# Graph layer on Trainium2: normalising two steps behind the statistics, ten loads issued by GpSimd, the first layer's bounds inside the input block, keys and values four chunks sooner

## The reference, cut to what matters

```
xn  = layernorm(x)
x0  = relu(gat(xn; W1, att1) + b1)        # 4 heads, softmax over the edges of each destination
x2  = gat(x0; W2, att2) + b2
mix = linear attention on xn: k, v normalised per head, dots = k^T v, q @ dots / N, then Wout, bout
x   = x + x2 + mix
x   = x + layernorm(x + top-2-of-16 experts(layernorm(x))) * gamma + beta
```

## Time and profile before

| | us |
|---|---|
| median of 3 runs (lowest, highest) | 2814.59 (2810.1, 2815.09) |
| the profiled execution | 2810.95 |
| its span, from first to last instruction | 2809.0 |
| POOL busy | 1864.1 (66%) |
| PE busy | 2204.9 (78%) |
| DVE busy | 1825.2 (65%) |
| ACT busy | 932.2 (33%) |
| largest group: 1568 gathers L957 | 1488.1, 949 ns each, 495.5 idle before them |

### The profile page before, as it was taken

How to read it: one execution, slowest core, us unless ns; L and a number is a source line. 1 busy time by engine, 2 the same in 40 slices (tenths; PEclk the granted TensorE clock), 3 DMA queues, 4 the chain that set the end, 5 groups by cost and what they waited for, 6 DMA issues and landing times. The chain is left out here.

```text
span 2809.0 us, 54426 instructions
## 1 busy us (share of the span) xinstructions
PE 2204.9 (78%) x11643; PEld 1733.5 (62%) x11644; DVE 1825.2 (65%) x4373; ACT 932.2 (33%) x2266; POOL 1864.1 (66%) x1942
## 2 busy tenths in 40 slices
PE   4638777777778777658888888888888479999986
PEld 3426555555555555446666666666666269999975
DVE  4767777777777777476666666666666565555546
ACT  3403333333333333202222222222222144444436
POOL 1447777777777777467777777777777126666654
PEclk9869999999999999879999999999999689999998
DMA  5535555555555555376565655565656345565546
GB/s 184 171 97 149 146 145 146 146 146 146 146 145 146 146 147 143 79 225 161 157 164 156 163 154 164 157 161 156 163 153 160 90 128 101 103 104 105 101 85 189
DMA packets 262987, 402.24 MB, mean 143 GB/s; under 512 B 78879, under 2 KB 175542, under 8 KB 262904
## 3 DMA queue, kind: packets, MB, share of 16 engines
q0 software_dynamic: 102880, 254.96, 36.8%
q1 hardware_dynamic: 122376, 105.98, 13.9%
q10 hardware_dynamic: 37663, 40.56, 4.4%
HBM read 347.09 MB, written 54.62 MB: 143 GB/s over the span
## 5 line engine op out<-in xcount | busy, mean ns | idle before, releaser
L957 POOL DMA_INDIRECT gathered<-table,idx x1568 | 1488.1, 949 | 495.5 <-issue 453.6
L1288 PE MATMUL psA_e<-scaled,hotf 128*128 128x260 f32 x3136 | 746.5, 392 | 44.0 <-issue 39.4
L1288 PEld LDWEIGHTS psA_e<-scaled,hotf 128*128 128x128 f32 x3136 | 589.4, 193 | 131.8 <-issue 48.2
L1159 ACT ACTIVATE scaled<-t_e 128x32 f32<-128x32 f32 x196 | 45.0, 230 | 733.8 <-DVE t_e L1021 722.9
L1691 POOL DMA_INDIRECT moe_d<-xscaled,xtarget x113 | 179.2, 1586 | 124.5 <-DVE xtarget L1635 52.0
L1032 DVE TENSOR_TENSOR scaled<-gathered,psDW_e 128x2048 f32<-128x2048 f32 x98 | 223.6, 2282 | 25.4 <-ACT psDW_e L1160 25.4
L1025 DVE TENSOR_TENSOR hotf<-psA_e,code_r 128x1024 f32<-128x1024 f32 x196 | 239.7, 1223 | 0.1
L1032 DVE TENSOR_TENSOR scaled<-gathered,psW_e 128x2048 f32<-128x2048 f32 x98 | 223.6, 2282 | 22.4 <-ACT psW_e L1160 22.4
L1663 PEld LDWEIGHTS xpsH<-xxT,w1e 128*128 128x128 f32 x1808 | 220.6, 193 | 6.1 <-ACT xxT L1592 0.4
L1672 PE MATMUL xpsO<-w,hidT 128*128 x904 | 216.8, 383 | 7.7 <-DVE hidT L1624 6.9
L1663 PE MATMUL xpsH<-xxT,w1e 128*128 128x128 f32 x1808 | 221.3, 276 | 0.0
(11 more groups left out here) (322 smaller groups left out, 3381.2 us busy)
## 6 DMA issues: line engine op xcount, KB each, us to landing
w<-codes_d SPq DMA_DIRECT2D x196, 256.0 KB
gathered<-table,idx POOLq DMA_INDIRECT x1592
w<-in_L_ffn_w ACTq DMA_DIRECT2D x8, 2048.0 KB, 19.1
xb<-in_L_ffn_b SPq DMA_DIRECT2D x113, 128.0 KB
table<-acc POOLq DMA_DIRECT2D x49, 130.0 KB
table<-acc ACTq DMA_DIRECT2D x49, 130.0 KB
xnT_d<-w SPq DMA_DIRECT2D x49, 128.0 KB, 2.5
w<-xnT_d SPq DMA_DIRECT2D x49, 128.0 KB, 3.8
```

The lines of the kernel that those rows point to most:

```text
L957: pool.indirect_dma_start(out=G[:, q, k, :], out_offset=None, in_=table, in_offset=bass.IndirectOffsetOnAxis(ap=idx[:, q, k:k + 1], axis=0 ...
L1159: act.activation(scaled[:, par, :, C:GW], t[:], ACT.Exp).then_inc(s["weights"], 1)
L1288: ins = pe.matmul(psA[:, q, 0:GW], hotf[:, q, k, :], scaled[:, par, k, :], start=(k == 0), stop=(k == KT - 1))
```

## The change

In `inputs`: (1) the normalising, and with it transpose, copy, store and product, stand one turn later. (2) Ten of the thirteen transfers move from ACT's list to POOL's, ahead of POOL's table stores; the same ten lines are gone from ACT's. (3) The body of `bounds` becomes a function, and for the first layer it runs at the end of DVE's list in the input block (with its two PE instructions at the end of PE's); the block `bounds` 0 is gone. In `gat_edges` 0: (4) all steps of keys and values have offsets smaller by four.

```diff
-                stage(bounds, 0, ident, ones, acc, dtab, own, peak, parts, wide, table[0], idx, G, firsts[0], None)
...
-            tiles(sp, (0, load), (3, store_x))
+            tiles(sp, (0, load), (4, store_x))
...
+            pool.wait_ge(s["filled"], 2)
+            pool.dma_start(by_chunk_i[0:FULL, :], a["dst"][0:FULL * CE].rearrange("(k e) -> k e", e=CE)).then_inc(s["dst_in"], 16)
+            pool.dma_start(by_chunk_i[FULL:NC, 0:REST * KT], a["dst"][FULL * CE:E].rearrange("(k e) -> k e", k=1)).then_inc(s["dst_in"], 16)
+            pool.dma_start(srcp[E:NC * CE].rearrange("(p t) -> p t", t=KT), zero_i[0:P - REST, :]).then_inc(s["src_stored"], 16)
+            pool.dma_start(srcp[0:E].rearrange("(p f) -> p f", p=P // 4), a["src"].rearrange("(p f) -> p f", p=P // 4)).then_inc(s["src_stored"], 16)
+            pool.dma_start(wkv[:], a["L0_mix_Wqkv"][MI:3 * MI, :].rearrange("(k p) c -> p k c", p=P)).then_inc(s["w_mix_in"], 16)
+            pool.dma_start(wout[:], a["L0_mix_Wout"].rearrange("(k p) c -> p k c", p=P)).then_inc(s["w_mix_in"], 16)
+            pool.dma_start(wq, a["L0_mix_Wqkv"][0:MI, :].rearrange("(k p) c -> p k c", p=P)).then_inc(s["w_mix_in"], 16)
+            pool.dma_start(wext1[:, :, 0:C], a["L0_gnn_W2"].rearrange("(k p) n -> p k n", p=P)).then_inc(s["w1_in"], 16)
+            pool.dma_start(att1[:, 0, :], a["L0_gnn_att_src2"].rearrange("(o h) c -> o (h c)", o=1).to_broadcast([P, C])).then_inc(s["w1_in"], 16)
+            pool.dma_start(att1[:, 1, :], a["L0_gnn_att_dst2"].rearrange("(o h) c -> o (h c)", o=1).to_broadcast([P, C])).then_inc(s["w1_in"], 16)
...
-            tiles(dve, (1, normalise), (0, stats))
+            tiles(dve, (2, normalise), (0, stats))
...
+            dve.wait_ge(s["h_out"], 2 * NT)
+            bound_values(dve, Chain(dve, s["bounds_steps"]), s, psH[:, 0], ident, acc, dtab, own, peak, parts, wide, places)
...
-            act.wait_ge(s["filled"], 2)
...
-            tiles(act, (0, root), (1, turned), (2, project))
+            tiles(act, (0, root), (2, turned), (3, project))
...
-            tiles(pe, (1, turn), (2, project))
+            tiles(pe, (2, turn), (3, project))
...
+            pe.wait_ge(s["ends"], 1)
+            pe.transpose(psH[0:2 * H, 0, 0:P], places[1][:], ident[:]).then_inc(s["bounds_turned"], 1)
+            pe.wait_ge(s["diagonal"], 1)
+            pe.matmul(psH[:, 0, 256:256 + 2 * H], ones[0:2 * H, :], places[3][:], start=True, stop=True).then_inc(s["bounds_spread"], 1)
...
-                rounds = chunks(sp, new_pass(sp), next_load, (0, load), (-1, load_codes), (1, load_x, True), head=SLOTS)
+                rounds = chunks(sp, new_pass(sp), next_load, (0, load), (-1, load_codes), (-3, load_x, True), head=SLOTS)
...
-                rounds = chunks(dve, both_new(dve), next_pass, (1, edge_logits), (1, placed), (1, edge_scale), (6, keys, True), (-1, one_hot), (2, own_terms), (3, gain), (5, denominators, True), (5, sums, True))
+                rounds = chunks(dve, both_new(dve), next_pass, (1, edge_logits), (1, placed), (1, edge_scale), (2, keys, True), (-1, one_hot), (2, own_terms), (3, gain), (5, denominators, True), (1, sums, True))
...
-                chunks(act, new_dest(act), nothing, (9, store, True), (6, roots, True), (1, exps), (6, divide, True), (5, squares, True), (7, relu, True), (8, copies, True))
+                chunks(act, new_dest(act), nothing, (9, store, True), (2, roots, True), (1, exps), (6, divide, True), (1, squares, True), (7, relu, True), (8, copies, True))
...
-                chunks(pe, nothing, nothing, (1, targets), (2, add), (7, fin_turn, True), (7, dots, True), (8, project, True),
-                       (1, after_logits), (5, keys, True), (4, values, True), (1, after_placed(2)))
+                chunks(pe, nothing, nothing, (1, targets), (2, add), (7, fin_turn, True), (3, dots, True), (8, project, True),
+                       (1, after_logits), (1, keys, True), (0, values, True), (1, after_placed(2)))
```

More of the change, by code:

```diff
@@ L237, in inputs, with bound_places @@
+def bound_places(sb):
+    return (sb("bd_low", [P, H]), sb("bd_ends", [P, 2 * H]), sb("bd_head", [2 * H, 1]), sb("bd_diag", [2 * H, 2 * H]), sb("bd_all", [P, 2 * H]),
+            sb("bd_spread", [P, H]), sb("bd_most", [P, 1]), sb("bd_rest", [P, NT + 2, H]))
 def inputs(nc, a, srcp, codes_d, xnT_d, table, partition, ident, identb, ones, iota, eps, code, lower, upper, first_tile, passes,
-           acc, dtab, dotsT, wext, attention_weights, spaces, idx, G, ahead, sem):
+           acc, dtab, dotsT, wext, attention_weights, spaces, idx, G, ahead, own, peak, parts, wide, sem):
@@ L283, in inputs @@
         psC = pb("psC", [P, 2, 512])
+        places = bound_places(sb)
         s = {n: sem("i_" + n) for n in ("x_in0", "x_in1", "x_in2", "x_in3", "xT_out0", "xT_out1", "xT_out2", "xT_out3", "xT_ps", "xT", "h_ps", "h_out",
@@ L536, in sb @@
             return ctx.enter_context(nc.sbuf_tensor(f"{name}_{layer}", shape, dt))
[L538 to L545, removed]
+        places = bound_places(sb)
+        ends, diag = places[1], places[3]
         ps = ctx.enter_context(nc.psum_tensor(f"bd_ps{layer}", [P, 512], F32))
@@ L550, in bounds @@
             psM = ctx.enter_context(nc.psum_tensor("bd_psM", [P, 512], F32))
-        s = {n: sem(f"bd{layer}_{n}") for n in ("steps", "ends", "turned", "diagonal", "spread", "values_mixed", "zmix", "queries_mixed", "mixM")}
+        s = {n: sem(f"bd{layer}_{n}") for n in ("steps", "ends", "bounds_turned", "diagonal", "bounds_spread", "values_mixed", "zmix", "queries_mixed", "mixM")}
         block = ctx.enter_context(nc.Block())
@@ L577, in _ @@
         def _(dve):
[L578 to L583, removed]
[L584 to L599 removed]
+            bound_values(dve, Chain(dve, s["steps"]), s, ps, ident, acc, dtab, own, peak, parts, wide, places)
         @block.tensor
@@ L607, in _ @@
             pe.wait_ge(s["ends"], 1)
-            pe.transpose(ps[0:2 * H, 0:P], ends[:], ident[:]).then_inc(s["turned"], 1)
+            pe.transpose(ps[0:2 * H, 0:P], ends[:], ident[:]).then_inc(s["bounds_turned"], 1)
             pe.wait_ge(s["diagonal"], 1)
-            pe.matmul(ps[:, 256:256 + 2 * H], ones[0:2 * H, :], diag[:], start=True, stop=True).then_inc(s["spread"], 1)
+            pe.matmul(ps[:, 256:256 + 2 * H], ones[0:2 * H, :], diag[:], start=True, stop=True).then_inc(s["bounds_spread"], 1)
             if mixing:
```

53 lines of the change are left out of this document (25 added, 28 removed).

## The result

| us | before | after |
|---|---|---|
| median (lowest, highest), runs on one chip | 2814.84 (2810.1, 2818.03), 4 | 2783.03 (2782.33, 2785.16), 4 |
| the profiled execution (its span) | 2810.95 (2809.0) | 2783.69 (2782.1) |

The ratio after to before is 0.989, 95% interval 0.9872 to 0.9907. Forecast were 2789, in a range of 2773 to 2803, and -24 us for the profiled execution against itself; it is -27.3 (span -26.9). The medians lie 31.8 us apart, 26 to 36 by the interval.

The account below looks back on a forecast made before the run. It took POOL's gathers to bound the middle of the edge block and one serial chain the path ahead of it. Terms -10 -3 +1 -7 +5 -10 = -24 us took 2810.95 to 2787; forecast 2789, range 2773 to 2803.

Parts of the forecast that it names:

- Start: Start of the input block: without the ten transfers on ACT the first reciprocal comes sooner; net gain 10 us, bounds 3.7 and 14.7.
- the price of 5 us: Input block: cost of the 2.3 MB of the ten transfers left for the tile loop; 5 us, between 0 and 11.
- Tiles: Tile loop of the input block: 0.07 us less on each of 44 turns, 3 us gained; bounds loss of 4, gain of 18.
- my rival of DVE's wait: Tile loop: DVE's wait for the root was the limit, turns shrink to 1.5 us, 11 us gained instead of 3; chance 0.15.
- the loads' cycle: Tile loop: chain from load to statistics, store and next load, 5.17 us for three turns, 1.72 each; claimed to stay.
- Drain: Behind the last tile's load: one more tile under way delays POOL's last stores by about 1 us.
- Bounds: End of the input block: bounds follow DVE's end and one block boundary goes; gain 7 us, bounds 6 and 8.
- Head: First turns of the edge block: keys and values ahead of own_terms delay POOL's gather; 5 us lost, between 0 and 9.
- End: Last turns of the edge block: keys and values already done, last store sooner; gain 10 us, bounds 13.5 and 5.
- TensorE's clock: End of the edge block: PE's clock may fall with less to do, so 10 us kept of a gain of 11.
- the rest: From the block behind the edge block to the end of the span; no change forecast, 0 us.
- the signs that I named: Expected marks in the changed profile, among them tiles 5 and 47 about 72 us apart, POOL's last-store wait about 3 us.

Follow-up runs that it names:

- e8: Changed kernel with POOL's ten transfers held until W1 and its attention vectors have landed; 2788.48 us, ratio to the kernel before 0.9912.
- e5: Changed kernel with SP's store of the normalised tile one turn further behind (offset 5 instead of 4); 2781.88 us, ratio to the kernel before 0.9891.
- e6: Changed kernel with ACT's copy of the transposed tile ahead of the next root in its list; 2783.4 us, ratio to the kernel before 0.9895.
- e9: Changed kernel with two extra TensorE products that nobody reads in the turn behind the last chunk; ratio to the kernel before 0.9894.
- e3: Kernel before with only the first layer's bounds moved to the end of the input block; ratio to the kernel before 0.9979.
- e7: Changed kernel with keys and values two chunks sooner than before instead of four; ratio to the kernel before 0.9898.
- e10: Changed kernel with the edits of e5 and e9 together and the keys behind own_terms in DVE's list; 2772.63 us, ratio to the kernel before 0.9871.
- e1: Kernel before with only the ten transfers moved from ACT to POOL; ratio to the kernel before 0.9947.
- e4: Kernel before with only keys and values four chunks sooner in the first layer's edge block; ratio to the kernel before 0.9988.
- the filler: Two extra TensorE products that nobody reads, added behind the last chunk; on the changed kernel (e9), last gather to next block 9.6 us instead of 12.3.
- e2: Kernel before with only the normalising two steps behind the statistics instead of one; ratio to the kernel before 0.9996.
- e12: Changed kernel with normalising back at one step behind, but the store one turn further behind it; ratio to the kernel before 0.9911.

## Why the prediction was right, point by point

- **Start, -10, measured -13.1.** The mechanism was right. Too large was the price of 5 us for the transfers that no longer hide behind ACT: they delay the reciprocal by 2.1 us (e8), and no delay behind it shows, since the turn in the loop stayed as it was.
- **Tiles, -3, measured -2.6, right by luck.** I put 0.07 us on each of 44 turns. The turns gained nothing (+0.4 in all). It is the first five tiles that gained 3.7, where x is in place and DVE's chain alone sets the pace: there my rival of DVE's wait was the truth, and behind it the loads' cycle was. The last load took 0.7 more. The spread at this mark is of the size of the term.
- **Why the loads' cycle stays.** The prediction saw that it would; e5 and e6 show what it consists of: a load stands behind a store, this behind ACT's copy, this behind the root of a tile whose load is just landing.
- **Drain, +1, measured 0.** One more tile under way delayed nothing on DVE. The forecast was about POOL's stores, and there the first gather stands 10.1 us behind the statistics of tile 48 instead of 8.9, 1.2 more; but kernels with one step have 8.2 to 9.9 and those with two 9.5 to 10.6, so that this is hardly told from none.
- **Bounds, -7, measured -6.9.** The mechanism was right: I had DVE and POOL end the input block together. They did, POOL last by 1.0 us (139.4 against 138.4). In e9, whose input block is the same, it was DVE by 0.2 (137.3 against 137.1). The other kernels fit. Where the bounds end 4.7 to 5.0 us behind POOL's last gather (changed, e3, e7, e8), the edge block starts 9.4 to 9.6 us behind that gather; where they end 6.2 behind it (e5, e6, e9, e10), it starts 4.1 to 4.2 behind the bounds. So the second step of the normalising had little to gain in the changed kernel. From e1's `upper` (130.70 + 0.34) and the 8.7 us from there to the end of the bounds I estimate that with one step DVE's queue would have drained at 140.0, against 139.4 for POOL's in the changed kernel. This combination was not run.
- **Head, +5, measured +4.9.** POOL's waits for L1043 make 3.5 of it (10.9 us instead of the 7.4 of the first 70 us before); the remaining 1.4 are spread and not assigned. e4 shows the same loss with the block at its old start. The sizes behind my 5 were too large for this chain. The values of tile 0 took 3.78 us at a granted clock of 0.50 (143 to 150 us), as I had it, but the scaling of chunk 0 comes only 0.5 us later behind the block's start, not 2. That of chunk 1 is another 1.8 later (I had 2.9 for sums and roots), `own_terms` another 1.0 (1.2 for the keys). This makes 3.4, and the close agreement with 5 needs the unassigned 1.4.
- **End, -10, measured -7.8.** The mis-sized part is TensorE's clock, for which I kept 1 us, as far as the filler shows it. Against the three kernels with the filler it cost 1.9 to 2.8 (10.4, 10.2 and 9.6 us instead of 12.3).

The two misses of the sum, 3 too little at the start and 2 too much at the end, partly cancel, which is luck; without the -1.3 of the rest it would be -25.6 against -24. Two of the signs that I named came out otherwise, without turning the argument: tiles 5 and 47 are 74.1 us apart, not 72, and the wait for the last store is 5.74, not 3. The median fell by 31.8 us, 5 more than the spans of the profiled runs; no stretch that the change touches shows these 5, and the spread behind the edge block is large enough for them.

## What to carry to other kernels

Read a change made in several places by marks on the path, and let each part run alone and in company: the second step of the normalising gains nothing measurable alone (e2), and is worth 7 us at tile 48 once the store no longer holds the loads (e5 against e12). When two engines end a block, read from its last rows which of them did, before you say that a gain on one is paid out. In a software pipeline look for in-order queues that tie a load to something unrelated, here a load behind a store behind a copy behind a root; moving one entry in the list by a turn was worth 8.9 us at tile 48. Work that is taken out of an engine's tail can lower TensorE's clock just where the tail is the path, as in the 2.97 us without work ahead of the granted 0.60 here.

## What the hardware showed that I had not expected

- The same transfer of Wout held ACT's sequencer 9.75 us as the ninth in a row and POOL's 0.73 us (L360). Two others of ACT's thirteen held it 5.87 (L428) and 3.18 us (L434), the other ten under 1.5 each. Whether ACT waited there for room in its queue was not tried.
- A load of 106 rows takes about twice as long as one of 128 (5.9 to 7.1 us to its statistics, against about 3), and in two pieces of 96 and 10 it takes no longer than the full one (3.1).
- TensorE's clock at the end of the edge block differs between kernels whose instructions there are the same (sixteen products in 4.3 to 6.7 us).
